# Keys and values of three attentions computed ahead, inside the first feed-forward, and kept in HBM

## The reference, cut to what matters

```
x = x + L0_xattn(ln(x), ctx)        # differential attention
x = x + L0_ffn(ln(x))               # two layers with quantised weights and activations
x = x + L1_xattn(ln(x), ctx, mask)  # plain attention, 16 heads of width 8
x = x + L1_ffn(ln(x))               # experts
x = x + L2_xattn(ln(x), ctx)        # plain attention
x = x + L2_ffn(ln(x))               # grouped experts
x = x + L3_xattn(ln(x), ctx)        # plain attention
x = x + L3_ffn(ln(x))               # experts with a capacity

# a plain attention, for each batch of 64 queries and 64 keys:
q, k, v = x @ Wq + bq, ctx @ Wk + bk, ctx @ Wv + bv   # split in 16 heads of 8
out = softmax(q k^T / sqrt(8)) v @ Wo + bo
```

## Time and profile before

| what | us |
|---|---|
| timed runs, median (lowest to highest) of 3 | 2234.18 (2232.45 to 2238.2) |
| profiled execution, its own time | 2232.57 |
| its span, first to last instruction | 2230.8 |
| second half of the first feed-forward | 447 to 584 in the span |
| loop of the first plain attention | 602 to 769 |
| loop of the second | 1063 to 1208 |
| loop of the third | 1749 to 1893 |

### The profile page before, as it was taken

One profiled execution on the slowest core, in us unless ns is written; L12 is line 12 of the kernel. 1 busy time (PEld: TensorE's weight loads), 2 busy tenths in 40 slices (PEclk: granted clock), 3 DMA queues, 4 the chain that ended last, 5 costly groups with the idle time before them and its releaser, 6 DMA issues. The chain is left out here.

```text
span 2230.8 us, 48391 instructions
## 1 busy us (share of the span) xinstructions
PE 1669.4 (75%) x14912; PEld 1187.2 (53%) x14915; DVE 1540.4 (69%) x3682; ACT 825.1 (37%) x1795; POOL 874.6 (39%) x1058
## 2 busy tenths in 40 slices
PE   3999962212499898996898699918999799358993
PEld 2777651011377665664677344417777577335552
DVE  4999976989677753437677899874555687863332
ACT  1544441344355422322564588700000465122221
POOL 1888841266144243005442000005554343027783
PEclk9999976555599889997898899958999799555555
DMA  3222200000000051111001477416774000424446
GB/s 111 68 66 66 65 17 28 0 0 1 7 1 0 16 162 42 40 36 40 1 0 34 151 311 297 198 37 224 282 265 161 7 0 1 120 47 81 81 83 143
DMA packets 178711, 183.56 MB, mean 82 GB/s; under 512 B 101378, under 2 KB 163650, under 8 KB 171202
## 3 DMA queue, kind: packets, MB, share of 16 engines
q1 hardware_dynamic: 154770, 111.88, 16.2%
q10 hardware_dynamic: 9520, 55.94, 7.1%
q0 software_dynamic: 14336, 14.69, 3.6%
HBM read 107.39 MB, written 72.45 MB: 81 GB/s over the span
## 5 line engine op out<-in xcount | busy, mean ns | idle before, releaser
L748 DVE TENSOR_REDUCE at_mx<-at_psS 128x16 f32<-128x1024 f32 x96 | 117.6, 1225 | 93.7 <-PE at_psS L653 93.7
L711 ACT ACTIVATE at_ET<-at_psT 128x512 f32<-128x512 f32 x192 | 114.6, 597 | 172.3 <-PE at_psT L662 171.7
L1922 POOL TENSOR_TENSOR gr_work<-gr_ring 128x512 f32<-128x512 f32 x96 | 121.7, 1280 | 104.3 <-DVE gr_work L1958 97.2
L617 POOL TENSOR_TENSOR at_KM<-at_K,at_mask 128x512 f32<-128x512 f32 x96 | 100.0, 1042 | 154.0 <-ACT at_Q L698 154.0
L2011 PEld LDWEIGHTS gr_psY<-gr_wd,gr_work 128*128 128x128 f32 x1024 | 134.8, 196 | 39.2 <-DVE gr_work L1958 22.8
L388 POOL TENSOR_TENSOR at_E<-at_Z,at_mx 128x512 f32<-128x512 f32 x128 | 130.9, 1044 | 50.1 <-DVE at_mx L513 50.1
L2011 PE MATMUL gr_psY<-gr_wd,gr_work 128*128 128x128 f32 x1024 | 142.4, 283 | 10.7 <-DVE gr_work L1958 10.6
L662 PE MATMUL at_psT<-kept_ident,at_Z 128*128 128x128 f32 x768 | 127.3, 289 | 9.6 <-DVE at_Z L761 4.6
L1844 PE MATMUL gr_psV<-kept_xT,gr_wu 128*128 (+1 forms) x256 | 125.9, 592 | 0.8 <-ACT gr_V L1713 0.8
L249 ACT ACT_TABLE_LOAD x6 | 7.7, 1283 | 314.7 <-PEq L63 299.3
L675 PE MATMUL at_psO<-at_VZ,at_ET 128*64 128x18 f32 x3072 | 106.9, 212 | 15.6 <-ACT at_ET L711 4.2
(11 more groups left out here) (554 smaller groups left out, 4631.9 us busy)
## 6 DMA issues: line engine op xcount, KB each, us to landing
gr_spill<-gr_ring SPq DMA_DIRECT2D x28, 1792.0 KB, 5.7
gr_ring<-gr_spill ACTq DMA_DIRECT2D x28, 1792.0 KB, 7.2
at_amask<-mask_Bx16xSxS_ff SPq DMA_DIRECT2D x128, 128.0 KB, 2.9
cap_acc<-cap_zero SPq DMA_DIRECT2D x2, 2112.0 KB, 12.6
cap_sums<-cap_acc SPq DMA_DIRECT2D x8, 512.0 KB, 7.2
ex_xs<-ex_zero SPq DMA_DIRECT2D x1, 2496.0 KB, 11.1
ex_row<-ex_xs SPq DMA_DIRECT2D x39, 64.0 KB, 1.8
ex_ys<-ex_out SPq DMA_DIRECT2D x39, 64.0 KB, 1.6
```

Source lines behind the costliest of these rows:

```text
L617: pool.tensor_tensor(KM[:, s, :, :], K[:, s, :].unsqueeze(1).broadcast_to([P, 4, P]), mask4[:, :].unsqueeze(2).broadcast_to([P, 4, P]), AL ...
L711: act.activation(ET[:, 4 * a:4 * a + 4, :].rearrange("p r q -> p (r q)"), psT[:, :], ACT.Exp, scale=QK_SCALE).then_inc(exped, 1)
L748: dve.tensor_reduce(mx[:, :].rearrange("p (g v) -> p g v", v=4), psS[:, :, 0:256].rearrange("p g (v k) -> p g v k", k=SEQ), AX.X, ALU.max) ...
L1922: pool.tensor_tensor(tp[:, s % 4, :], ring[:, s // 4, first, :], ring[:, s // 4, first + 1, :], ALU.mult).then_inc(pooled, 1)
```

## The change

`bit_ffn` gets the key and value weights and the key biases of L1, L2 and L3 (nine more loads ahead of its block), and a stage for each pair of tiles in its second half: TensorE computes the transposed keys of the three layers for 256 tokens and the values of the three layers for each of two tiles of 128 tokens, ScalarE copies them into KS and VS (VS has VZ's layout, with zeros and ones set once by GpSimd), and SyncE writes both to HBM with three DMAs a pair. `attention_rows` no longer has cst, Wk, Wv, the key bias, `project_v`, `take_v` and the memsets of VZ; SyncE loads K (64 KB) and VZ (144 KB) of each tile, four tiles deep, the first four in the layer norm's block ahead.

```
@@ attention_rows @@
+    SLOTS = 4
-        cst = sb("cst", [P, 2, 2, 2, SEQ])
-        Q, K = sb("Q", [P, 2, P]), sb("K", [P, 2, P])
+        Q, K = sb("Q", [P, 2, P]), sb("K", [P, SLOTS, P])
-        VZ = sb("VZ", [P, 2 * PAIRS, 2, DH + 1])
+        VZ = sb("VZ", [P, SLOTS, 2 * PAIRS, 2, DH + 1])
+        def load_keys(sp, i, s):
+            sp.dma_start(K[:, s, :], keys[:, bass.ds(P * i, P)]).then_inc(k_in[s], 16)
+        def load_values(sp, i, s):
+            v = VZ[:, s, :, :, :].rearrange("p r j w -> p (r j w)")
+            sp.dma_start(v, values[bass.ds(i, 1), :, :].rearrange("a p w -> p (a w)")).then_inc(v_in[s], 16)
         def loads(sp):
...
+            for i in range(SLOTS):
+                load_keys(sp, i, i)
+                load_values(sp, i, i)
+            @block.sync
+            def _(sp):
+                def load_ahead(i, s, n):
+                    if isinstance(i, int) and i < SLOTS:
+                        return
+                    sp.wait_ge(km_ready, i - (SLOTS - 1))
+                    load_keys(sp, i, s)
+                    sp.wait_ge(summed, i - (SLOTS - 1))
+                    load_values(sp, i, s)
+                run(sp, [(0, load_ahead)])
                 def part_heads(i, s, n):
-                    pool.wait_ge(qk_taken, 2 * i + 2)
+                    pool.wait_ge(k_in[s], 16 * n + 16)
                     wait_past(pool, scored, i - 1)
-                run(pool, [(1, stage_ctx), (1, part_heads)])
+                run(pool, [(1, part_heads), (1, add_bias)])
+                def project_q(i, s, n):
+                    wait_past(pe, q_taken, i)
+                    pe.matmul(psP[:, 0:P], Wq[:, :], m.xT[:, bass.ds(P * i, P)], start=True, stop=True).then_inc(q_done, 1)
                 def score(i, s, n):
                     pe.wait_ge(km_ready, i + 1)
+                    pe.wait_ge(q_taken, i + 1)
                 def weigh(i, s, n):
                     pe.wait_ge(exped, 2 * i + 2)
-                    pe.wait_ge(v_taken, 2 * i + 2)
+                    pe.wait_ge(v_in[s], 16 * n + 16)
-                run(pe, [(-1, weigh), (0, turn(0)), (-2, project_out), (0, project_v), (1, score), (0, turn(1)), (-1, turn_o), (2, project_qk)])
+                run(pe, [(-1, weigh), (0, turn(0)), (-2, project_out), (1, score), (0, turn(1)), (-1, turn_o), (2, project_q)])
-                run(act, [(1, take_qk), (-2, take_o), (0, exponent(0)), (0, take_v), (0, exponent(1))])
+                run(act, [(1, take_q), (-2, take_o), (0, exponent(0)), (0, exponent(1))])
-                chain.link(dve.memset(VZ[:, :, :, :], 0.0))
@@ bit_ffn @@
+        LAYERS, VW = len(wks), 2 * HEADS // 2 * (DH + 1)
+            for l in range(LAYERS):
+                sp.dma_start(kw[:, l, :], wks[l]).then_inc(loaded, 16)
+                sp.dma_start(vw[:, l, :], wvs[l]).then_inc(loaded, 16)
+                sp.dma_start(kb[:, l:l + 1], bks[l].rearrange("(p a) -> p a", a=1)).then_inc(loaded, 16)
-        LOADS = 16 * 8
+        LOADS = 16 * (8 + 3 * LAYERS)
+                def write_kv(k, s, n):
+                    u = s % 2
+                    sp.wait_ge(kv_taken, k + 1)
+                    sp.dma_start(keys[:, :, bass.ds(2 * P * k, 2 * P)].rearrange("l p w -> p l w"), KS[:, u, :, :]).then_inc(kv_out[u], 16)
+                    for b in range(2):
+                        dst = values[bass.ds(2 * k, 2), :, :, b * VW:b * VW + VW].rearrange("i l (t k) w -> k (i l) t w", t=2)
+                        sp.dma_start(dst, VS[64 * b:64 * b + 64, u, :, :, :]).then_inc(kv_out[u], 16)
+                pipelined(sp, PAIRS, [(0, write_kv)], period=4)
+                for u in range(2):
+                    sp.wait_ge(kv_out[u], 48 * PAIRS // 2)
+                def take_kv(k, s, n):
+                    u = s % 2
+                    act.wait_ge(projected, k + 1)
+                    wait_past(act, kv_out[u], 48 * (2 * n + s // 2))
+                    for l in range(LAYERS):
+                        act.activation(KS[:, u, l, :], keys_at(l), ACT.Identity, bias=kb[:, l:l + 1])
+                    for i in range(2):
+                        v = psH[:, 2 + i, 0:LAYERS * D].rearrange("p (l r j d) -> p l r j d", l=LAYERS, j=2, d=DH)
+                        for j in range(2):
+                            mine = VS[:, u, LAYERS * i:LAYERS * i + LAYERS, j, :].rearrange("p l (r w) -> p l r w", w=2 * DH + 2)
+                            last = act.activation(mine[:, :, :, j * (DH + 1):j * (DH + 1) + DH], v[:, :, :, j, :], ACT.Copy)
+                    last.then_inc(kv_taken, 1)
-                pipelined(act, PAIRS, [(-1, take_h), (2, normalise), (0, to_integers)], period=4)
+                pipelined(act, PAIRS, [(-1, take_h), (2, normalise), (0, to_integers), (0, take_kv)], period=4)
+                def project_kv(k, s, n):
+                    wait_past(pe, kv_taken, k)
+                    for l in range(LAYERS):
+                        pe.matmul(keys_at(l), kw[:, l, :], m.ctxT[:, bass.ds(2 * P * k, 2 * P)], start=True, stop=True)
+                    for i in range(2):
+                        last = pe.matmul(psH[:, 2 + i, 0:LAYERS * D], m.ctxT[:, bass.ds(P * (2 * k + i), P)],
+                                         vw[:, :, :].rearrange("p l d -> p (l d)"), start=True, stop=True)
+                    last.then_inc(projected, 1)
-                pipelined(pe, PAIRS, [(-1, down), (0, turn_h)], period=4)
+                pipelined(pe, PAIRS, [(-1, down), (0, turn_h), (1, project_kv)], period=4)
@@ program @@
+        keys = nc.dram_tensor("kv_keys", (len(wks), P, TOK), F32, kind="Internal").ap()
+        values = nc.dram_tensor("kv_values", (NT, len(wvs), P, 2 * HEADS * (DH + 1)), F32, kind="Internal").ap()
+        bit_ffn(nc, m, t, wks, wvs, bks, keys, values)
```

More of the change, by code:

```diff
@@ L626, in _ @@
                 pe.wait_ge(prepared, 2)
-                pe.wait_ge(m.ctx_in, 16)
-                def project_qk(i, s, n):
-                    wait_past(pe, v_taken, 2 * (i - 1))
-                    wait_past(pe, qk_taken, 2 * i)
-                    pe.matmul(psP[:, 0:P], Wq[:, :], m.xT[:, bass.ds(P * i, P)], start=True, stop=True)
-                    pe.matmul(psP[:, P:2 * P], Wk[:, :], m.ctxT[:, bass.ds(P * i, P)], start=True, stop=True).then_inc(qk_done, 1)
-                def project_v(i, s, n):
-                    pe.wait_ge(staged, i + 1)
-                    pe.wait_ge(qk_taken, 2 * at_most(i + 2))
-                    for b in range(2):
-                        last = pe.matmul(psP[:, 256 + b * P:256 + b * P + P], cst[:, s, b, :, :].rearrange("p t k -> p (t k)"),
-                                         Wv[:, :], start=True, stop=True)
-                    last.then_inc(v_done, 1)
+                def project_q(i, s, n):
+                    wait_past(pe, q_taken, i)
+                    pe.matmul(psP[:, 0:P], Wq[:, :], m.xT[:, bass.ds(P * i, P)], start=True, stop=True).then_inc(q_done, 1)
                 def score(i, s, n):
                     pe.wait_ge(km_ready, i + 1)
+                    pe.wait_ge(q_taken, i + 1)
                     wait_past(pe, shifted, 2 * i)
@@ L652, in score @@
                             chans = slice(32 * g, 32 * g + 32)
-                            last = pe.matmul(psS[rows, g, 0:256], Q[chans, s, rows], KM[chans, s, :, rows],
+                            last = pe.matmul(psS[rows, g, 0:256], Q[chans, s % 2, rows], KM[chans, s % 2, :, rows],
                                              start=keep_mask is None, stop=True)
@@ L692, in _, with take_q @@
                 act.wait_ge(prepared, 2)
[L694 to L695 removed]
+                def take_q(i, s, n):
+                    act.wait_ge(q_done, i + 1)
                     wait_past(act, scored, i - 1)
[L697 to L705 removed]
+                    act.activation(Q[:, s % 2, :], psP[:, 0:P], ACT.Identity, bias=bqc[:, 0:1]).then_inc(q_taken, 1)
                 def exponent(a):
@@ L956, in bit_ffn, with _ @@
         PAIRS = NT // 2
-        LOADS = 16 * 8
+        LOADS = 16 * (8 + 3 * LAYERS)
+        cleared, projected, kv_taken = m.sem("cleared"), m.sem("projected"), m.sem("kv_taken")
+        kv_out = [m.sem(f"kv_out{u}") for u in range(2)]
+        keys_at = lambda l: psH[:, l // 2, 2 * P * (l % 2):2 * P * (l % 2) + 2 * P]
         with nc.Block() as block:
+            @block.sync
+            def _(sp):
+                def write_kv(k, s, n):
[8 more added lines that the diff above has]
+                    sp.wait_ge(kv_out[u], 48 * PAIRS // 2)
             @block.vector
```

67 lines of the change are left out of this document (28 added, 39 removed).

## The result

The changed kernel takes 2216.57 us (median of 4 runs, 2214.85 to 2223.47), the kernel before 2236.19 in the runs beside it (4, 2232.45 to 2238.23): a ratio of 0.9925 with a 95% interval of 0.9906 to 0.9945. Faster, as forecast, but by 20 us and not by 47: 2187 was forecast, 2213 the top of the range. The profiled execution took 2223.47 us (span 2221.7), the slowest of the four.

A forecast was written before the change was run, and what follows sets the result against it. TensorE's order of work was taken to bound the attention loops. Terms +3 - 9 + 4 - 5.5 - 11.5 - 28 = -47 us took the profiled 2232.57 to 2185.6, with the median of runs 2187; range 2168 to 2213.

The forecast's parts named there:

- Wk is worth nothing: Attention loops: removing Wk's matmul gains nothing, since `weigh` behind it waits for ACT's exponent anyway.
- V's slot: Attention loops: removing `project_v` from PE saves 0.44 us a tile, -28 us over two loops; upper bound 0.65 a tile.
- B: Attentions run down to the floor of the score loop, 3.65 us a tile: 2171 us; chance 0.13.
- C: Attentions: a wait takes half of V's slot, 0.2 us a tile, -19 for -39.5: 2208 us; chance 0.12.
- the beginning: Start of the first feed-forward: nine more loads in front of DVE's wait cost +3 us, lower bound 0.5.
- the end: End of the feed-forward's second half: the last pair's `take_kv`, issues and landing add +4 us (+1 to +10).
- I take 6.9: Feed-forward's second half: a pair takes 6.9 us instead of 7.51, over 15 steps -9 us.
- The ring: Second half: way over projections, `down`, residual, quantising, conversion and copies, 16.8 us for two pairs at the low clock.
- so I expect it to rise: Second half: PE's clock goes high, as its work stands nearly side by side, 7.3 of 8.4 us at the low clock.
- POOL now starts on one pair at a time, so DVE stands less than before: Second half: DVE's standing beside POOL's work shrinks; no size of its own, part of the 6.9 us a pair.
- Rival A: Second half: the clock stays low, 8.4 us a pair, +13 for -9, 2209 us in all; chance 0.17.
- Rival D: Second half: writes hold `take_kv` through kv_out, +150 for -9, about 2346 us; chance 0.05.

The follow-up runs named there:

- 7: Changed kernel with a dummy matmul of Wk's size put back behind the queries' in the attentions: 2211.86 us.
- 8: Changed kernel with two dummy matmuls of V's size in V's old slot, with that slot's wait for the queries: 2251.45 us.
- 5: Changed kernel with `take_kv` and `project_kv` one pair further ahead: 2207.16 us, ratio 0.9877.
- 14: Changed kernel with `take_kv` and `project_kv` one pair ahead, loads inside the block, VS clearing later, and `down` ahead of `project_kv`: 2188.03 us, ratio 0.9809.
- 2: Kernel before with the new feed-forward stage but without `project_kv`, attentions still making their own keys and values: 2246.54 us.
- 12: Changed kernel with copies and projections one pair ahead, loads inside the block, VS clearing later, and keys moved to the feed-forward's first half: 2198.04 us, ratio 0.9834.
- 16: Kernel of 12 with `take_kv` moved ahead of the conversion `to_integers`: 2197.99 us, ratio 0.9846.

## Why the prediction was wrong

**Right: the attentions.** "Wk is worth nothing" (7), V's slot carries the gain (8), tiles of 4.55 and 3.92 us for 4.55 and 3.87, the wait ahead of `weigh` 0.54 for "about 0.5", loads covered, the starts shorter: -13.0 and -14.1 us for -13.3 and -15.8. The third gave -7.6: half of its gain went into a start at the low clock, a term that the prediction did not have. Rivals B and C fall: 3.92 is neither the floor of 3.65 nor half the slot.

**Near, in part by luck: the beginning**, +2.4 us for +3. The issues were the whole of the term and cost some 0.5 us, its lower bound; the other 1.9 are the clearing of VS, which the prediction did not have.

**Wrong by size: the end.** +7.1 us for +4. `take_kv` came late as well: it waited for projections at the low clock (2.67 us ahead of L1157), then issues, a landing of 5.5 and the barrier. It lay within the bounds of +1 to +10 (the prediction's own terms, 10 to 13 against 6, give 4 to 7, and it took the lower end), and 5 shows that all of it was to be had back.

**Wrong: the second half**, the step "I take 6.9", -9 us against a measured +9.7. The ring in it was right, the clock in the ring was not, and DVE was not counted.
- The prediction added up this ring at the low clock: projections 5.1, `down` 1.1, residual 1.05, meeting POOL 2.3, quantising 3.5, conversion and copies 3.75, together 16.8 us for two pairs. The round from 490.68 to 506.80 has 16.1: conversion and copies 3.2, projections 5.5, then `down`, the residual at 500.20, and a quantising with one standing of 2.06, until 506.76. The forecast rests on the same walk with projections of 2.55 us. The step that failed is "so I expect it to rise": it rose for the second pair of each round (2.85 us), but the first pair, the one in the ring, took 4.5 to 5.5, since TensorE stands for 3 to 6.5 us between rounds.
- What this costs is DVE's wait for `down`, a term that the forecast had at nothing: 1.7 us a pair, 21.6 of 100 us. With `down` first it is gone, and 7.23 a pair remain (14).
- "POOL now starts on one pair at a time, so DVE stands less than before" came true, 2.0 us a pair for 3.2. But the walk let DVE stand once and weighed only ACT's fill. DVE's own work is 4.5 us a pair, and in every kernel with both of POOL's operations where it hardly waits (before, 2, 12, 14 and 16) the pair is 7.2 to 7.8 us. So 6.9 would have been short even at the high clock; how short is open, since no run changed the clock alone.

ACT's load was right (2.2 us of copies for 2.6, the pair 6.0 for 6.3), and so was PE's, 2.85 us at the high clock for 2.55 and 5.5 at the low for 5.1.

**Rival A**, the low clock, named the cause, and its 8.4 a pair is near 8.16. Its condition was put too strongly: the mean clock is 0.76, not 0.5, since only one of the two projections in a round is slow. The rule of the Trainium skill ("TensorE: Matmul & The Clock Gate", "HAM oscillation — how this bites in real kernels"), that waits between groups of matmuls throttle the clock anew in every round, holds for the first pair of every round here and is paid there; the second has the high clock. **Rival D** falls: nothing waited for the writes, at 188 GB/s in the busiest 10 us.

**The sum.** Against the forecast the second half costs 19 us, the end 3, the third attention 8. The 6 us ahead of the feed-forward belong to this execution, which is 7 us above the median. That the best order (14) comes to 2188.03, near the 2187 forecast for another kernel, is two errors apart: its stage is still 7.23 a pair, and it has both repairs.

## What to carry to other kernels

Before work is moved into a stage because its engine idles there, find the engine that has no time left in that stage (here VectorE, 4.5 us of own work and 3.2 of standing a pair) and ask what the new work makes it wait for. Follow the ring that sets the rhythm once round, with the standing in and with each matmul at the clock that it will have after the gap ahead of it. In a list in order, put new work behind the step for which another engine waits: exchanging `down` and `project_kv`, one line, was worth 12.7 us by the medians (2200.75 to 2188.03; 12.4 in the stage) of the 28.5 between the changed kernel and the best. Give the last unit's copies and writes a lead of one, and keep loads that are needed late out of the wait at the start.
